# Pairwise bilinear products: where the 128 rows of a store lie in its block of the output

## The chip, the cores and the metric

The kernel runs on one core of one Trainium2 chip. Times are microseconds (us) on the device for one execution, as the median of several runs; a lower time is better.

## The reference: what is computed

`x` holds 4096 samples of 32 fields of 64 numbers, `W` is 64 x 64. Every field is multiplied by `W`, and then every pair of fields i < j gives one elementwise product, 496 pairs a sample:

```python
vid = jnp.einsum('bfd,de->bfe', x, W)
idx_i, idx_j = jnp.triu_indices(F_, k=1)
return x[:, idx_i, :] * vid[:, idx_j, :]
```

All numbers are 32-bit floats. The result has 4096 x 496 x 64 elements, 520 million bytes, against 33.6 million bytes of input.

## The kernel before, in words

**Layout.** The host gives the kernel `x` transposed: the 128 partitions are two halves of the batch times 64 numbers of a field, and a partition holds, tile by tile, 32 fields of 128 samples each. One field of one tile, 128 floats or 512 bytes in a partition, is called a unit. There are 16 tiles (`NT`), each giving 496 units of output in every partition, so 7936 units in all.

**The memory.** One buffer `mem` of 445 units a partition holds input and output. Inputs live in its low units: tiles 0 to 7 are loaded at the start, tiles 8 to 15 later as a second group (`GROUPS`, function `load`).

**The stages of a tile.** TensorE multiplies the 32 fields by a block-diagonal copy of `W` into `vid` (line 319), in two halves of 16 fields. VectorE multiplies fields of `x` with fields of `vid` (line 299), several units in one instruction, and writes the products into `mem`. The order of the pairs within a tile is by blocks (`by_block`), and the host puts them into the reference's order afterwards.

**The stores.** The 7936 units are cut into 74 slots, written out by hand in the table `SLOTS`: for each the number of units (51 to 128) and its home in `mem`. As soon as the last unit of a slot has been written, `store` (line 258) issues one DMA for it: 128 rows, one a partition, each of as many units as the slot has. The first 46 slots (`SECOND`) are issued from SP, the others from ACT; each queue takes its stores in the order of the slots. An issue waits for the semaphore `made`, which VectorE raises with each of its instructions. VectorE in turn, before it writes into units of `mem`, waits for the stores that still read them (`after`, line 201). The eight loads go through SP as well.

**The output in HBM.** It is one array of 7936 x 128 rows of one unit. Slot after slot has a block of it (`BLOCKS`), which it fills without gaps: within the block, partition p's units follow partition p - 1's. The host cuts the blocks apart and joins them again.

The function that the change touches is `store`, which hands the two sides of the DMA to `transfer` (line 194), whose line 196 issues it:

```python
rows = out[BLOCKS[slot] : BLOCKS[slot + 1], :].rearrange("(p u) c -> p u c", p=P)
transfer(rows[:, : end - begin, :], mem[:, units[0] : units[1], :], units, True, needs, act if slot >= SECOND else sp)
```

Of the kernel before, what the change touches and what calls it, by code (L numbers as in the profile page):

```python
# [10 lines left out]
P = 128  # L11

C = 128
# [27 lines left out]

SECOND = 46

PAD = 24
# [6 lines left out]
def row(n):  # L53

    return n
# [3 lines left out]
BLOCKS = [0, *accumulate(P * row(n) for n, *_ in SLOTS)]  # L59
# [112 lines left out]
def pairwise_bilinear_kernel(nc, x0, x, out):  # L172
# [8 lines left out]
    mem = ctx.enter_context(nc.sbuf_tensor([P, UNITS, C], F32))  # L181
# [8 lines left out]
    sp, act, dve = (Queue(engine, behind) for engine in (nc.sync, nc.scalar, nc.vector))  # L190
# [3 lines left out]
    def transfer(out_, in_, units, reads, needs, queue=sp):  # L194
        sem = nc.alloc_semaphore(f"moved{len(moved)}")
        queue.issue(lambda: queue.engine.dma_start(out=out_, in_=in_), needs).then_inc(sem, 16)  # L196
        queue.note(sem, 16)
        moved.append((units, reads, sem))
        return sem

    def after(units):

        needs = [(s, 16) for u, reads, s in moved if reads and overlap(u, units)]
        last = max((n for spans, n in worked if any(overlap(units, s) for s in spans)), default=0)
        return needs + [(made, last)] * (last > 0)
# [52 lines left out]
    def store(slot, last):  # L258
        nonlocal hold
        begin, end = STARTS[slot : slot + 2]  # L260
        home = SLOTS[slot][1]
        units = (home, home + end - begin)
        needs = [(made, last)]
        if hold:
            needs.append((hold[-2], 16))
            hold = []
        rows = out[BLOCKS[slot] : BLOCKS[slot + 1], :].rearrange("(p u) c -> p u c", p=P)
        transfer(rows[:, : end - begin, :], mem[:, units[0] : units[1], :], units, True, needs, act if slot >= SECOND else sp)

    for t in range(NT):
        if t in begins[1:]:
            hold = load(begins.index(t))
            for late in held:
                store(*late)
            held = []
        xs = (place_of(t, F), place_of(t, F) + F)
        blocks = list(products(by_block(), t * NP))
        for k, (at, n, nest, i, j) in enumerate(blocks):
            slot = bisect_right(STARTS, at) - 1  # L280
            begin, end = STARTS[slot], STARTS[slot + 1]
            home = SLOTS[slot][1]
            units = (home + at - begin, home + at - begin + n)
# [11 lines left out]
            needs = [(there, 2 * t + 2 - high), *after(units)]  # L295
# [9 lines left out]
            if at == end:  # L305
                late = (slot, counts[made])
                group = sum(behind <= slot for behind in STRETCHES)
                if t < begins[group]:
                    held.append(late)
                else:  # L310
                    store(*late)
# [65 lines left out]
```

How the kernel before makes its waits and increments, by code:

```python
    def issue(self, make, needs):  # L148
        needs = self.waits(needs)
        for sem, n in needs[:-1]:
            self.engine.wait_ge(sem, n)
        instruction = make()
        for sem, n in needs[-1:]:
            instruction.wait_op(sem, n, "sem-ge")
        return instruction
# [16 lines left out]
def pairwise_bilinear_kernel(nc, x0, x, out):  # L172
# [50 lines left out]
            (place + HALF, place + F + 1), False, [],  # L223
        ),
        transfer(mem[:, place : place + HALF, :], x0[:, :HALF, :], (place, place + HALF), False, []),
    ]
    work(lambda: nc.vector.memset(w2[:, :], 0.0), [], [], made)
    for half in (slice(0, D), slice(D, P)):
        work(
            lambda: nc.vector.tensor_copy(w2[half, half], mem[half, place + F, :D]),
            [(place + F, place + F + 1)], [(first[0], 16), (made, 1)], made,
        )
    nc.vector.wait_ge(made, 3).then_inc(free, 1)
    nc.vector.wait_ge(first[1], 16).then_inc(free, 1)
    owed = 0
# [67 lines left out]
            at += n  # L304
            if at == end:
                late = (slot, counts[made])
                group = sum(behind <= slot for behind in STRETCHES)
                if t < begins[group]:
                    held.append(late)
                else:
                    store(*late)
    for sem, n in sp.waits([(sem, 16) for _, _, sem in moved]):
        nc.sync.wait_ge(sem, n)
    def half(xt, lo):
        nc.tensor.wait_ge(free, 1).then_inc(free, -1)
```

## Time and profile before

| | |
|---|---|
| Median of 3 runs | 1284.6 us (1284.49 to 1284.81) |
| The profiled execution | span 1282.6 us, first to last instruction |
| VectorE busy | 1079.9 us, 273 instructions |
| TensorE busy (matmul) | 179.4 us |
| Bytes moved | 553.70 MB: 33.59 read from HBM, 520.09 written |
| Mean rate | 432 GB/s |

For the profiled execution the trace gives the span alone; the runs' median lies 2.0 us above it, which is what lies around the first and the last instruction. Read the table from the bytes: a span of 1282.6 us at 432 GB/s is all of the 553.70 MB, so data moved from the first slice to the last. VectorE is the busiest of the engines and stands still for a sixth of the span.

### The profile page before, as it was taken

To read this page: it belongs to the slowest core of one execution; us is meant where nothing else is said; L and a number is where in the kernel's file an instruction comes from. 1 tells how busy PE (TensorE), PEld (TensorE's weight loads), DVE (VectorE), ACT (ScalarE), POOL (GpSimd) and SP (SyncE) were. 2 spreads that over 40 slices of the span, in tenths; PEclk is the share of its full clock that TensorE was granted. 3 is DMA by queue.
4 is the path that set the end of the run, shared out by engine and by line. 5 is a ranking of instruction groups with operands and counts; after the bars stand their busy time and mean duration, and the time that the engine had idled before them with its cause. 6 is when DMAs were issued, how large, how long until landed. Compare 5 with 4: busy or idle time off the path is not lost. (4 is left out here: it accounts for less than half of the span.)

```text
span 1282.6 us, 1255 instructions
## 1 busy us (share of the span) xinstructions
PE 179.4 (14%) x256; PEld 70.2 (5%) x256; DVE 1079.9 (84%) x273; POOL 0.2 (0%) x4
## 2 busy tenths in 40 slices
PE   2011120301111030300020111103020020201100
PEld 1000000100000010100010000001010010100000
DVE  6589989988897989998027989989988899899980
POOL 0000000000000000000000000000000000000000
PEclk8566565756656565655565655656556575656555
DMA  9999999999999999999999999999999999999999
GB/s 404 423 435 435 438 433 433 439 435 425 435 444 429 425 437 442 428 425 446 416 426 437 426 433 436 438 434 434 439 431 442 421 437 435 427 446 429 434 425 409
DMA packets 11810, 553.70 MB, mean 432 GB/s; under 512 B 1312, under 2 KB 1312, under 8 KB 1312
## 3 DMA queue, kind: packets, MB, share of 16 engines
q1 hardware_dynamic: 7776, 340.30, 61.5%
q10 hardware_dynamic: 4032, 213.39, 38.4%
q14 instruction: 2, 0.02, 0.0%
HBM read 33.59 MB, written 520.09 MB: 432 GB/s over the span
## 5 line engine op out<-in xcount | busy, mean ns | idle before, releaser
L299 DVE TENSOR_TENSOR mem<-mem,vid 128x1024 f32<-128x1024 f32 (+11 forms) x270 | 1079.3, 4065 | 161.2 <-DMA out_dram<-mem 114.5
L319 PE MATMUL vid<-mem,w 128*128 x256 | 179.4, 866 | 1016.1 <-PEq L317 1016.1
L319 PEld LDWEIGHTS vid<-mem,w 128*128 128x128 f32 x256 | 70.2, 288 | 1124.4 <-issue 1124.4
L230 DVE COPY w<-mem 64x64 f32<-64x64 f32 x2 | 0.4, 191 | 5.1 <-DMA mem<-in_r_x_dram 5.0
L227 DVE MEMSET w<- 128x128 f32 x1 | 0.2, 165 | 0.8 <-PEq L344 0.8
L344 POOL MEMSET const-bfloat16-1.0<- 128x1 bf16 x1 | 0.1, 101 | 0.0
L344 POOL MEMSET const-uint8-127<- 128x1 uint8 x1 | 0.1, 101 | 0.0
L344 POOL MEMSET const-float32-0.0<- 128x1 f32 x1 | 0.1, 98 | 0.2 <-issue 0.2
L344 POOL MEMSET const-float32-1.0<- 128x1 f32 x1 | 0.1, 98 | 0.0
## 6 DMA issues: line engine op xcount, KB each, us to landing
out_dram<-mem ACTq DMA_DIRECT2D x9, 7680.0 KB, 23.3
out_dram<-mem SPq DMA_DIRECT2D x4, 6656.0 KB, 20.5
out_dram<-mem SPq DMA_DIRECT2D x3, 7680.0 KB, 23.1
out_dram<-mem ACTq DMA_DIRECT2D x3, 7168.0 KB, 21.5
out_dram<-mem SPq DMA_DIRECT2D x5, 4096.0 KB, 17.5
out_dram<-mem SPq DMA_DIRECT2D x3, 5632.0 KB, 18.4
out_dram<-mem SPq DMA_DIRECT2D x3, 5120.0 KB, 17.3
out_dram<-mem SPq DMA_DIRECT2D x2, 7168.0 KB, 22.6
```

The costliest lines, as they stand in the source:

```text
L227: work(lambda: nc.vector.memset(w2[:, :], 0.0), [], [], made)
L230: lambda: nc.vector.tensor_copy(w2[half, half], mem[half, place + F, :D]),
L299: lambda: nc.vector.tensor_tensor(o, left, right, ALU.mult),
L319: last = nc.tensor.matmul(vid[:, b : b + BANK, :], lhsT=w2[:, :], rhs=xt(b), start=True, stop=True)
L344: nc = _bacc.Bacc("TRN2", target_bir_lowering=False, num_devices=1, dynamic_dma_scratch_size=512)
```

## The change

The place of a row within its slot's block of the output is another. Row p is written as p = 8e + k, with e from 0 to 15 and k from 0 to 7. Before, it lay at place p of the block, that is 8e + k; now it lies at place 16k + e. The DMA's output side so has an outermost dimension of 16 (e), then one of 8 (k), then the row. The input side, 128 partitions of `mem`, is as it was. The host undoes the new order when it joins the blocks. All 74 stores are changed alike; the loads are not.

```diff
+RUN = 8
...
-        rows = out[BLOCKS[slot] : BLOCKS[slot + 1], :].rearrange("(p u) c -> p u c", p=P)
-        transfer(rows[:, : end - begin, :], mem[:, units[0] : units[1], :], units, True, needs, act if slot >= SECOND else sp)
+        rows = out[BLOCKS[slot] : BLOCKS[slot + 1], :].rearrange("(k e u) c -> e k u c", k=RUN, e=P // RUN)
+        transfer(rows, mem[:, units[0] : units[1], :], units, True, needs, act if slot >= SECOND else sp)
...
-    got = [got[a:b].reshape(P, -1, C)[:, :n] for a, b, (n, *_) in zip(BLOCKS, BLOCKS[1:], SLOTS)]
+    got = [
+        got[a:b].reshape(RUN, P // RUN, n, C).transpose(1, 0, 2, 3).reshape(P, n, C)
+        for a, b, (n, *_) in zip(BLOCKS, BLOCKS[1:], SLOTS)
+    ]
```

The program's order on SP's queue shows the forms. First the kernel before, the last two loads and the first six stores (sizes are the output side's, in elements; `in_r_x_dram` is the input):

```order
L196 DMA mem<-in_r_x_dram 128x8960
L196 DMA mem<-in_r_x_dram 128x3328
L196 DMA out_dram<-mem 128x10240
L196 DMA out_dram<-mem 128x13952
L196 DMA out_dram<-mem 128x10624
L196 DMA out_dram<-mem 128x7168
L196 DMA out_dram<-mem 128x8192
L196 DMA out_dram<-mem 128x10240
```

Then the same place in the changed kernel, where the added constant shifts the line numbers by three:

```order
L199 DMA mem<-in_r_x_dram 128x8960
L199 DMA mem<-in_r_x_dram 128x3328
L199 DMA out_dram<-mem 16x8x10240
L199 DMA out_dram<-mem 16x8x13952
L199 DMA out_dram<-mem 16x8x10624
L199 DMA out_dram<-mem 16x8x7168
L199 DMA out_dram<-mem 16x8x8192
L199 DMA out_dram<-mem 16x8x10240
```

Nothing has moved: each store is where it was, with a row as long as before, and its 128 rows are counted as 16 x 8. On ACT's queue, and on the engines, it is the same.

## Rows read from the trace of the kernel before

**Rows 1.** The page, part 1: busy us of each engine, share of the span, instructions.

```profile
span 1282.6 us, 1255 instructions
...
PE 179.4 (14%) x256; PEld 70.2 (5%) x256; DVE 1079.9 (84%) x273; POOL 0.2 (0%) x4
```

**Rows 2.** The page, part 2: DMA busy tenths and rate in 40 slices.

```profile
DMA  9999999999999999999999999999999999999999
GB/s 404 423 435 435 438 433 433 439 435 425 435 444 429 425 437 442 428 425 446 416 426 437 426 433 436 438 434 434 439 431 442 421 437 435 427 446 429 434 425 409
DMA packets 11810, 553.70 MB, mean 432 GB/s; under 512 B 1312, under 2 KB 1312, under 8 KB 1312
```

**Rows 3.** The page, part 3: DMA queues; packets, MB, share of 16 engines' span.

```profile
q1 hardware_dynamic: 7776, 340.30, 61.5%
q10 hardware_dynamic: 4032, 213.39, 38.4%
...
HBM read 33.59 MB, written 520.09 MB: 432 GB/s over the span
```

**Rows 4.** Busy time in stretches; the last two columns are DMA share and GB/s.

```profile
0.00:32.00 32.00, 8.59 (x16) 3.58 (x16) 20.28 (x9) 0.20 (x4) 0.82 0.96 404
64.00:192.00 128.00, 24.20 (x32) 9.27 (x32) 114.10 (x39) 0.00 (x0) 0.58 1.01 435
192.00:320.00 128.00, 16.87 (x24) 6.56 (x24) 119.80 (x32) 0.00 (x0) 0.58 1.01 436
320.00:448.00 128.00, 16.26 (x24) 6.39 (x24) 115.84 (x26) 0.00 (x0) 0.58 1.00 434
448.00:576.00 128.00, 23.22 (x32) 9.08 (x32) 124.14 (x25) 0.00 (x0) 0.59 1.00 434
768.00:896.00 128.00, 23.61 (x32) 9.16 (x32) 120.82 (x37) 0.00 (x0) 0.57 1.00 434
896.00:1024.00 128.00, 11.51 (x16) 4.47 (x16) 114.96 (x27) 0.00 (x0) 0.55 1.00 435
1024.00:1152.00 128.00, 22.67 (x32) 8.92 (x32) 117.51 (x31) 0.00 (x0) 0.59 1.01 435
1247.00:1283.00 36.00, 0.00 (x0) 0.00 (x0) 0.00 (x0) 0.00 (x0) 0.50 0.92 397
```

**Rows 5.** Waits of DVE, then of SP: us in total, times, longest.

```profile
DVE mem L299 <- DMA out_dram<-mem: 114.5, 35, 18.3
DVE mem L299 <- PE vid L319: 46.5, 2, 40.7
...
SPq L196 <- DVE mem L299: 695.0, 44, 48.9
SPq L151 <- DMA out_dram<-mem: 17.9, 1, 17.9
```

**Rows 6.** DMA issues: stores of the 26 slots of 128 units, median us to landing.

```profile
out_dram<-mem SPq DMA_DIRECT2D x15, 26.5
out_dram<-mem ACTq DMA_DIRECT2D x11, 25.6
```

**Rows 7.** All DMA issues of line 196: ns min/median/max of one issue; last, landing of stores.

```profile
L196 SPq DMA_DIRECT2D out_dram<-mem x46: 332/332/431, 38.5 to 773.7; - x46
L196 ACTq DMA_DIRECT2D out_dram<-mem x28: 338/338/380, 785.1 to 1247.0; - x28
L196 SPq DMA_DIRECT2D mem<-in_r_x_dram x8: 328/425/1252, 0.7 to 672.8; - x8
...
DMA to landing us min/median/max: 15.0/23.0/38.0
```

**Rows 8.** DVE at line 299, the largest shape: busy us, mean ns of one.

```profile
L299 DVE TENSOR_TENSOR mem<-mem,vid 128x16384 f32<-128x16384 f32 x5 | 86.0, 17211 | 0.0
```

## The prediction

> **What bounds the kernel now.** I read the views from the outside in: the page's engines, then the DMA slices, the queues, the stretches, the waits, and last the single DMA issues. VectorE looks busiest, 1079.9 us or 84% of the span [rows 1]. But the DMA engines stand at 9 tenths or more in every one of the 40 slices, and the rate never leaves 404 to 446 GB/s [rows 2]. The queues say it more sharply: packets of the two queues fill 61.5% and 38.4% of sixteen engines' span, 99.9% together [rows 3]. There is no idle DMA time to win. VectorE waits 114.5 us for stores, PE's product delays it for 46.5 us, and SP waits 695.0 us for VectorE to finish a slot [rows 5]; all of this lies beside transfers that go on. The bound is the time that one DMA engine (I call it a lane) needs for its rows, added up over its rows.
>
> That pace can be worked out. The second queue carries stores alone, 213.39 MB in 38.4% of 1282.6 us, which is 492.5 us: 433.3 GB/s, or 27.1 GB/s a lane [rows 3]. It hardly depends on anything. The seven stretches of 128 us give 434 to 436 GB/s with a DMA share of 1.00 to 1.01, with short slots and long ones, from SP's queue and from ACT's [rows 4]. A row of 128 units (65,536 bytes) at 27.1 GB/s takes 2.42 us.
>
> **The change, part by part.** The reshaping of the result on the host is outside the measured time. On the chip nothing is added, removed or moved: 74 stores and 8 loads are issued before [rows 7], and the order printed above keeps every one at its place and on its queue. Line and engine counts, semaphores and waits stay. Only the output side of the 74 stores changes: 128 rows become 16 x 8 rows. The loads (33.59 MB read) keep their form. An issue costs its sequencer some 0.33 us [rows 7]; even if the extra dimension doubled it, 74 x 0.33 = 24 us would lie on SP and ACT, beside the DMA, since an issue takes 23.0 us to land while the next one is already there [rows 7]. I cost that at nothing; what covers it is the rest of the store in flight, and without that cover it could cost 24 us at most.
>
> What is left is the traffic itself, and two things about it are new.
>
> First, the places. Rows 8e to 8e + 7 used to be neighbours in HBM; now the rows 8e + k of all sixteen e are. The pace in [rows 4] is the same for all slot sizes, so nothing in HBM shows as a limit now. The most that better places can give is the best stretch everywhere: 553.70 MB at 436 GB/s is 1269.9 us, 12.7 us less than the span. I take 0.
>
 No row of the trace of before shows two lanes at one port, so the price has to be bounded. From below, it is the 12.7 us gain just named. From above, every store takes twice its time. The stores are 520.09 MB [rows 3], at 433.3 GB/s 1200.3 us, so the rest of the span is 82.3 us (33.59 MB of loads at the first queue's 431.4 GB/s are 77.9 us, and gaps). Twice 1200.3 and 82.3 make 2482.9 us; the runs' median of 1284.6 us lies 2.0 us over the span, so 2484.9 us.
>
> I take a value near the upper end, because of what the evenness in [rows 2 to 4] means: the bound is a fixed pace on the way from the chip's memory to a lane, not a shared pool that averages out, and the change rearranges that very side.
>
> How near depends on how well two lanes keep step. Say that a pair shares one port for four rows, and another for the next four. If one of them leads by x rows, x of four go alone and 4 - x at half speed: 8 - x row times instead of 4. With fair sharing a lead neither grows nor shrinks. The end of the run bounds it: in the last 36 us the DMA share is 0.92 [rows 4], so lanes stand empty for 2.9 us on average, the last receipt included, or 1.2 rows of 2.42 us. So x lies between 0 and 1.2; I take a third of that, 0.4, since the receipt is part of it. The factor is 7.6 / 4 = 1.9: 1200.3 x 1.9 = 2280.6, plus 82.3, plus 2.0, is **2365 us**. With x = 1.2 the factor is 1.7, which gives 2125 us. The upper end takes the 17.9 us that SP waits at the change of the tile groups [rows 5], stores twice as slow lengthening it by as much again: 2503, rounded to 2505 us.
>
> The Trainium skill has this geometry. "DMA: Bandwidth & Descriptors", section "The descriptor swizzle", says that in a transfer of 128 partitions each engine is given two blocks of four partitions that belong to one port, with no port shared; it lists other shapes separately. "SBUF — State Buffer", section "Door 1: The DMA port swizzle", puts partitions 0 to 3 and 32 to 35 on one port, so that lanes e and e + 4 would pair, and gives 27.2 GB/s to a port; the 27.1 GB/s of a lane in [rows 3] agrees with that number, but no row shows which port it was. Its table has 64 partitions, half the ports, at 196 GB/s against 328 for all of them, for loads of 1 MiB; by that ratio of 1.67 the stores would come out at 2009 us and the whole, as an estimate, at 2093.
>
> VectorE is no second bound then: its 1079.9 us fit into 2365 us twice over. Its longest operation, 17.2 us [rows 8], delays a store only if the queue runs dry, which slower stores make rarer.
>
> **The rivals.**
> - *The lanes meet, but drift apart.* If the sharing is not fair, one lane of a pair runs ahead until it is four rows in front, and then nobody shares. For it: nothing couples the lanes but the stores' completions, and a 128-unit store takes 25.6 to 26.5 us to land where its own transfer takes 19.4 [rows 6], so a lane has some 6 to 7 us, nearly three rows, of queue to run ahead in. Against it: the same number says that there is little more, so a full four rows of lead are hard to reach. With x = 2.5 the factor is 1.375, and the time 1735 us; the case covers 1300 to 2125.
> - *No two lanes meet* (the other side: not slower). The dealing stays as it is, or a port can feed two lanes. The place is the same read side, the price 0, and it decides if a lane's 27.1 GB/s is its own limit and not that of what it reads from. For it: the queues' 99.9% cannot tell a lane's limit from a port's. Then the time is 1284.6 us, or, if neighbouring places also suit the HBM better, 1272 to 1282. The Trainium skill speaks for the latter in "DMA: Bandwidth & Descriptors", section "Latency and other measured facts": rows 512 KiB apart gave 207 GB/s a direction where a padded pitch gave 214. The trace doesn't agree that it happens here: a 128-unit slot has its rows eight apart at that distance, and the stretches that are full of such slots run as fast as the others [rows 4].
> - *Neighbouring places get in each other's way in HBM.* Sixteen lanes now write one stretch of sixteen rows. If that cost a twentieth of the stores' pace, it would be 1200.3 / 20 = 60 us, so 1345 us. Nothing in the profile speaks for it.
>
> **How the numbers follow.** Lanes meet and stay nearly in step: 0.55, with 2125 to 2505 as its own range. They meet and drift: 0.20. HBM loses: 0.05. No two meet and the time stays within 0.2% (about what a measurement of this kernel can tell from no change): 0.13. It gains: 0.07. So slower 0.80, same 0.13, faster 0.07. The forecast is the likeliest case, 2365 us. The range has to take in the first three cases to hold 8 times in 10, from 1290 to 2505 us.
>
> **What would show it.** If I am right, the DMA share stays near 1.00 in all 40 slices while the rate falls to 225 to 260 GB/s wherever stores run, and stays above 400 GB/s in the first 32 us, where loads run (404 before [rows 4]). The two queues still fill nearly the whole span. The landing of a 128-unit store goes from 26 us to over 45. VectorE's busy time stays at 1080 us and its wait for stores grows from 114.5 us to over 1000, its wait for PE all but vanishing. The forecast is wrong if packets still take 2.42 us for 65,536 bytes, that is, if the rate stays at 432 GB/s; the drift shows as a rate that climbs through the run.

## The result, and the profile after

The changed kernel takes 2159.9 us (2150.1 to 2173.6, six runs), the kernel before 1284.4 us beside it. The ratio is 1.682, with a 95% interval of 1.678 to 1.686: clearly slower, by 875.5 us.

First the page of the changed kernel: its engines, the DMA slices, the queues. They answer to [rows 1 to 3].

```profile
span 2158.7 us, 1255 instructions
...
PE 182.5 (8%) x256; PEld 71.4 (3%) x256; DVE 1082.5 (50%) x273; POOL 0.2 (0%) x4
...
DMA  9999999999999999999859998999999999999996
GB/s 372 233 290 295 251 240 262 241 237 241 251 250 250 243 250 262 273 284 295 311 165 247 276 297 216 233 242 280 245 255 247 242 258 261 231 247 250 275 282 183
...
q1 hardware_dynamic: 7776, 340.30, 57.8%
q10 hardware_dynamic: 4032, 213.39, 38.5%
```

VectorE is busy for as long as before (1082.5 us), yet the span has grown by 876.1 us. The DMA engines stand at 9 tenths nearly everywhere, as before, but what they move in a slice has fallen from 404 to 446 GB/s to 230 to 310 in most of them. So it is the packets that take longer. The stores' second queue shows it without any loads in between: 38.5% of 2158.7 us is 831.1 us for the same 213.39 MB that took 492.5 us [rows 3], a factor of 1.69.

The two queues' shares split the loss in two. Together they fill 96.3% of the span, 2078.8 us, where they filled 99.9%, 1281.3 us, before: packets are 797.5 us longer. The remaining 3.7% are 79.9 us of empty lanes, where there were 1.3. The sum, 797.5 and 78.6, is the 876.1 us.

Stretches of the changed kernel (columns as in [rows 4]; DMA share and GB/s last):

```profile
0.00:32.00 32.00, 8.64 (x16) 3.60 (x16) 20.34 (x9) 0.20 (x4) 0.82 0.96 405
60.00:90.00 30.00, 0.00 (x0) 0.00 (x0) 11.08 (x5) 0.00 (x0) 0.50 1.02 230
90.00:120.00 30.00, 6.04 (x8) 2.36 (x8) 14.61 (x4) 0.00 (x0) 0.56 0.96 243
120.00:150.00 30.00, 6.01 (x8) 2.37 (x8) 19.27 (x6) 0.00 (x0) 0.56 1.02 307
150.00:180.00 30.00, 0.00 (x0) 0.00 (x0) 22.03 (x7) 0.00 (x0) 0.50 0.92 330
180.00:210.00 30.00, 0.00 (x0) 0.00 (x0) 18.65 (x8) 0.00 (x0) 0.50 1.00 263
270.00:300.00 30.00, 0.00 (x0) 0.00 (x0) 15.81 (x6) 0.00 (x0) 0.50 0.97 235
320.00:576.00 256.00, 23.36 (x32) 9.15 (x32) 128.04 (x36) 0.00 (x0) 0.54 0.98 246
1120.00:1150.00 30.00, 0.00 (x0) 0.00 (x0) 11.18 (x5) 0.00 (x0) 0.50 0.93 206
1150.00:1180.00 30.00, 0.00 (x0) 0.00 (x0) 16.70 (x4) 0.00 (x0) 0.50 1.00 254
1180.00:1210.00 30.00, 5.11 (x8) 2.02 (x8) 20.90 (x7) 0.00 (x0) 0.61 1.01 289
1270.00:1300.00 30.00, 0.00 (x0) 0.00 (x0) 23.63 (x6) 0.00 (x0) 0.50 1.00 310
1600.00:1856.00 256.00, 19.18 (x29) 7.59 (x28) 131.28 (x36) 0.00 (x0) 0.55 0.98 250
2112.00:2158.00 46.00, 0.00 (x0) 0.00 (x0) 0.00 (x0) 0.00 (x0) 0.50 0.54 163
```

The first 32 us, full of loads, run at 405 GB/s as before (404). The stores that follow start at 230 GB/s, and the rate then climbs to 330 from the stretch at 60 us to that at 150 us. It doesn't stay there: 263 in the next stretch, 235 at 270 us. It climbs again after 1120 us, where the second group of tiles begins: 206, 254, 289, and 310 at 1270 us. In the long stretches it is near 250. At the very end the share is 0.54, so lanes finish far apart: 46 us times 0.46 is 21 us of empty lanes on average, against 2.9 before [rows 4].

The traces also keep each row's packet and each lane's landing, one by one. In the kernel before, all 1408 rows of the second queue's 128-unit stores take 2.42 to 2.46 us. In the changed kernel a quarter of them (345) still take under 2.6 us, and over half (822) take 4.4 us or more, up to 5.36: a row mostly goes at the full pace or at about half of it. The time between the first and the last of a store's sixteen landings is at most 2.0 us in all stores but one before. In the changed kernel it grows through the first eight stores, 1.1, 3.7, 6.1, 7.8, 9.7, 12.0, 13.5 and 14.9 us, then falls to 8.3; later it is up to 50. So lanes do get ahead of others, and not for good.

The waits of VectorE, and then SP's wait at the change of the tile groups, which answer to [rows 5]:

```profile
DVE mem L302 <- DMA out_dram<-mem: 933.9, 62, 45.0
DVE mem L302 <- PE vid L322: 61.1, 2, 55.2
```

```profile
SPq L154 <- DMA out_dram<-mem: 44.4, 1, 44.4
```

It waits 933.9 us for stores, where it waited 114.5: it now spends nearly as long waiting for room in the memory as working. Its two waits for PE, a short one at the start and 55.2 us at the change of the tile groups, are 61.1 us and not the 46.5 of before: at the change SP holds the loads back for 44.4 us, until the stores that still use the place have landed, where it was 17.9. (The upper end of the forecast had that wait doubled, to 36.)

And the issues of the stores, then the landing of the 26 slots of 128 units, which answer to [rows 7] and [rows 6]:

```profile
L199 SPq DMA_DIRECT2D out_dram<-mem x46: 538/538/625, 38.3 to 1276.0; - x46
L199 ACTq DMA_DIRECT2D out_dram<-mem x28: 545/546/607, 1287.4 to 2083.7; - x28
...
DMA to landing us min/median/max: 26.3/51.6/84.5
```

```profile
out_dram<-mem SPq DMA_DIRECT2D x15, 64.5
out_dram<-mem ACTq DMA_DIRECT2D x11, 55.4
```

The issue costs 0.54 us where it cost 0.33, and the landing of a 128-unit store 55 to 65 us where it took 26.

### The profile page after: what moved, and what is told of

Its sections match the earlier page's. It is cut to its first block and busy times, and to the rows that moved or that the text cites. A ratio compares the mean times of both kernels' runs of the same rounds, so it can differ in the third digit from the quotient of the medians.

```text
span 2158.7 us, 1255 instructions
## 1 busy us (share of the span) xinstructions
PE 182.5 (8%) x256; PEld 71.4 (3%) x256; DVE 1082.5 (50%) x273; POOL 0.2 (0%) x4
## 2 busy tenths in 40 slices
DMA packets 11810, 553.70 MB, mean 256 GB/s; under 512 B 1312, under 2 KB 1312, under 8 KB 1312
## 3 DMA queue, kind: packets, MB, share of 16 engines
q10 hardware_dynamic: 4032, 213.39, 38.5%
## 5 line engine op out<-in xcount | busy, mean ns | idle before, releaser
L302 DVE TENSOR_TENSOR mem<-mem,vid 128x1024 f32<-128x1024 f32 (+11 forms) x270 | 1081.9, 4068 | 995.4 <-DMA out_dram<-mem 933.9
## 6 DMA issues: line engine op xcount, KB each, us to landing
out_dram<-mem SPq DMA_DIRECT2D x4, 6656.0 KB, 35.5
```

The source lines that it names most:

```text
L302: lambda: nc.vector.tensor_tensor(o, left, right, ALU.mult),
```

## The experiments

Theory A: two lanes read through one port, because each now has eight consecutive partitions. Theory B: neighbouring places get in each other's way in HBM. The change moved two things together; the first two runs move one each.

**The dealing alone.** Rows at their old places, with gaps that keep the form of 16 x 8 rows (the gaps leave the output's content as it is; the host skips them):

```diff
-BLOCKS = [0, *accumulate(P * row(n) for n, *_ in SLOTS)]
+BLOCKS = [0, *accumulate(P * n + 16 for n, *_ in SLOTS)]
...
+        rows = out[BLOCKS[slot] : BLOCKS[slot + 1], :].rearrange("(e w) c -> e w c", e=16)
+        rows = rows[:, : 8 * (end - begin), :].rearrange("e (k u) c -> e k u c", k=8)
...
```

> The dealing of the changed kernel with the places of the kernel before: row 8e + k lies at place 8e + k again, but each group of eight rows is followed by one unit of gap, so that the output side keeps its form of 16 x 8 rows. Theory A (two lanes read through one port, since a lane has eight consecutive partitions): as slow as the change, 2100 to 2220 us. Theory B (the sixteen neighbouring places get in each other's way in HBM): the time of the kernel before, 1280 to 1300 us.

Measured: 2158.4 us, ratio 1.681 (1.676 to 1.685). Its page shows the rate and the queues:

```profile
GB/s 374 232 288 275 252 248 265 243 230 240 253 251 258 241 248 259 264 279 273 303 213 230 282 288 231 228 240 280 247 255 245 242 259 258 239 245 260 273 295 194
...
q1 hardware_dynamic: 7776, 340.30, 58.4%
q10 hardware_dynamic: 4032, 213.39, 38.4%
```

These are the changed kernel's numbers, down to the climb in the third and fourth slices. The new dealing by itself has the whole price: 2158.4 us with the old places, 2159.9 with the new.

**The places alone.** 128 rows outermost as before, each cut in eight:

```diff
+        cut = 8 if (end - begin) % 8 == 0 else 1
+        rows = out[BLOCKS[slot] : BLOCKS[slot + 1], :].rearrange("(j p u) c -> p j u c", j=cut, p=P)
...
```

> The dealing of the kernel before (128 rows outermost) with neighbouring places: a row is cut into eight pieces, and piece j of row p lies at place 128j + p, so that the lanes write one stretch at a time, about as long as in the changed kernel (slots whose units do not divide by eight stay as they were). Theory A (ports): the time of the kernel before and a few per cent for shorter descriptors, 1284 to 1330 us. Theory B (places): near the change, 1900 us or more.

Measured: 1332.8 us, ratio 1.038 (1.036 to 1.040), 2.8 us above the range given for theory A and far from B's.

**The same pieces in order** is the control that this number asked for:

```diff
-BLOCKS = [0, *accumulate(P * row(n) for n, *_ in SLOTS)]
+BLOCKS = [0, *accumulate(P * (n + (9 if n % 8 == 0 else 0)) for n, *_ in SLOTS)]
...
+        rows = out[BLOCKS[slot] : BLOCKS[slot + 1], :].rearrange("(p w) c -> p w c", p=P)
+        if cut > 1:
+            rows = rows[:, :-1, :]
+        rows = rows.rearrange("p (j u) c -> p j u c", j=cut)[:, :, : n // cut, :]
...
```

> The control for the run with the places alone: the same eight pieces a row, but at the places of the kernel before, with one unit of gap after each piece and one more after each row, so that the output side has the same form. If the 3.8% of that run are the price of the short descriptors: 1325 to 1340 us. If they are the price of neighbouring places: 1284 to 1300 us.

Measured: 1332.4 us, ratio 1.037 (1.035 to 1.039). The page's packets and queues, first with neighbouring places, then in order:

```profile
DMA packets 70946, 553.70 MB, mean 416 GB/s; under 512 B 1312, under 2 KB 1312, under 8 KB 42272
...
q1 hardware_dynamic: 43616, 340.30, 61.7%
q10 hardware_dynamic: 27328, 213.39, 38.7%
```

```profile
DMA packets 70946, 553.70 MB, mean 416 GB/s; under 512 B 1312, under 2 KB 1312, under 8 KB 42272
...
q1 hardware_dynamic: 43616, 340.30, 61.7%
q10 hardware_dynamic: 27328, 213.39, 38.7%
```

Same packets, same shares, same time to 0.4 us. So the 3.8% are the price of cutting rows, and neighbouring places cost nothing in this form. Theory B falls.

**Two halves of the partitions**, places as before and no 16 x 8 anywhere:

```diff
-        transfer(rows[:, : end - begin, :], mem[:, units[0] : units[1], :], units, True, needs, act if slot >= SECOND else sp)
+        both = [
+            (rows[part, : end - begin, :], mem[part, units[0] : units[1], :])
+            for part in (slice(0, 64), slice(64, P))
+        ]
+        transfer(both, None, units, True, needs, act if slot >= SECOND else sp)
...
```

> Places as before, but each store is two issues, partitions 0 to 63 and then 64 to 127, each with 64 rows outermost on both sides. The half issues reach half of the ports, so sixteen lanes must share them two by two, in a form without 16 x 8. Theory A (ports): slow like the change, 2050 to 2490 us. Theory B (places), and theory C (the form of 16 x 8 itself is slow to issue or to walk): 1284 to 1310 us.

Measured: 2165.3 us, ratio 1.686 (1.683 to 1.690). **The control** cuts the units in two and not the partitions:

```diff
...
+            for lo, hi in ((0, n // 2), (n // 2, n))
...
```

> The control for two issues a store: all 128 partitions in both, the first half of the units and then the second. All theories: 1284 to 1300 us, the shorter descriptors and twice the issues costing 1% at most. If it is much slower, the run with two halves says nothing on ports.

Measured: 1291.7 us, ratio 1.006 (1.004 to 1.008). Packets and queues of the two, halves of the partitions first:

```profile
DMA packets 12995, 553.72 MB, mean 255 GB/s; under 512 B 2496, under 2 KB 2496, under 8 KB 2496
...
q1 hardware_dynamic: 8512, 340.30, 57.8%
q10 hardware_dynamic: 4480, 213.39, 38.2%
```

```profile
DMA packets 22467, 553.72 MB, mean 429 GB/s; under 512 B 2496, under 2 KB 2496, under 8 KB 2496
...
q1 hardware_dynamic: 14400, 340.30, 61.6%
q10 hardware_dynamic: 8064, 213.39, 38.5%
```

The issues are as many in both. The one that reaches 64 partitions at a time is slow like the change, in a form that has nothing of it but the partitions that lanes read at one time. So it is neither the form of 16 x 8 nor its costlier issue.

**How many lanes, or where they read?** The next two runs use fewer lanes, each store waiting for the one before it:

```diff
-RUN = 8
+RUN = 64
...
-        needs = [(made, last)]
+        needs = [(made, last)] + [(sem, 16) for _, reads, sem in moved if reads][-1:]
```

> The changed kernel in step, with the output side as 2 x 64 rows (row 64e + k at place 2k + e): two lanes with 64 consecutive partitions each, which by theory A read from different halves of the ports and share none. Both theories A (ports) and D (a lane slows with the number of lanes in use, wherever they read): the lane's own pace, 27.1 GB/s: 54 GB/s in all, some 9700 us.

The other has `RUN = 32`, which makes four lanes:

> The same with 4 x 32 rows: four lanes with 32 consecutive partitions each; by theory A lanes 0 and 1 meet at every port of one half, 2 and 3 of the other, with a lead growing within a store. Theory A (ports): four lanes bring little, 27.1 GB/s times 2 to 3: 6500 to 9700 us. Without shared ports (theory D, or none): four times 27.1 GB/s, 108 GB/s, 4900 to 5000 us.

Measured: 9810.0 us with two lanes, 9170.4 with four (one run each). The rates in 40 slices, two lanes first:

```profile
GB/s 113 53 53 54 54 53 54 53 54 53 54 53 54 53 53 54 53 54 53 107 60 53 53 53 53 54 54 53 54 53 54 53 54 54 53 53 54 54 54 53
```

```profile
GB/s 122 59 61 57 56 59 58 55 57 57 59 55 58 55 57 58 55 57 56 109 69 60 57 60 56 57 57 59 57 57 56 58 58 56 57 55 57 57 56 57
```

Slices at 100 and more, and the one of 60 or 69, hold the loads. The two queues' packets fill 13.1% of sixteen engines' span (8.1 and 5.0) in the first run and 25.0% (15.0 and 10.0) in the second: two lanes of sixteen would be 12.5% and four 25.0%, so the outermost dimension does set how many lanes a store uses, and they are nearly always busy. Outside the loads two lanes move 53 to 54 GB/s, 27 each, the pace of a lane in the kernel before. Four lanes move 55 to 61 GB/s together, about 14 each. Sixteen lanes moved 433 with the old dealing, so it is not their number: a lane with partitions 0 to 31 and one with 32 to 63 share what they read through, and one with 0 to 63 beside one with 64 to 127 does not. (These two runs alone would also allow 0 to 31 to share with 96 to 127; but then the run with two halves, where all lanes read the same half, would have been fast.)

The Trainium skill says just this in "SBUF — State Buffer", section "Door 1: The DMA port swizzle": partitions p and p + 32 lie behind one port, and p + 64 behind another. The two runs agree with it; no run names the ports, nor shows which lanes pair in the changed kernel.

**Why 1.69 and not twice?** Theory A1 says that leads grow from store to store. Here every store of the changed kernel waits for the one before it (the second `needs` line above, with `RUN = 8`), so that no lead is carried on:

> The changed kernel, where each store is issued only when the store before it has landed, so that all lanes begin each store together and no lane can carry a lead over. Theory A1 (a pair shares its port, and the change is faster than twice the stores' time because leads build up from store to store): the stores come near twice their time, 1.85 to 2.0 times 1200 us, and 74 landings of 2 to 3 us each come on top: 2450 to 2700 us. Theory A2 (leads do not matter, and the sharing itself costs 1.73 times): 1.73 times 1200, 82, and the landings: 2300 to 2400 us.

And the kernel before with the same wait:

> The control: the kernel before with the same wait of each store for the one before it. Both theories: 1284 us and 74 bubbles of 2 to 4 us each, 1430 to 1600 us. The difference to the run of the change in step is what the dealing costs when no lane leads: about 1000 to 1200 us by theory A1, 870 by A2.

Measured: 2701.9 us, 1.9 above the range of theory A1, against 1393.4 us, below the 1430 given for the control. The queues, and the landing of a 128-unit store, of the change in step:

```profile
q1 hardware_dynamic: 7776, 340.30, 56.2%
q10 hardware_dynamic: 4032, 213.39, 37.3%
```

```profile
out_dram<-mem SPq DMA_DIRECT2D x15, 42.0
```

and of the kernel before in step:

```profile
q1 hardware_dynamic: 7776, 340.30, 56.9%
q10 hardware_dynamic: 4032, 213.39, 35.5%
```

```profile
out_dram<-mem SPq DMA_DIRECT2D x15, 20.7
```

The second queue's packets take 37.3% of 2701.1 us, 1007.5 us, against 35.5% of 1392.2, 494.2 us: a factor of 2.04. In the kernel before the wait leaves the packets as they were (494.2 against 492.5 us). The landing says the same, 42.0 against 20.7 us. The control's bubbles were smaller than I gave, 109 us in 74 stores or 1.5 us each, and the difference of 1308.5 us is above the 1000 to 1200 that I gave for A1 and far above the 870 of A2. It is made of 1239 us in packets (93.5% of 2701.1 against 92.4% of 1392.2) and 70 us in empty lanes. Row by row: none of the second queue's 128-unit rows is under 3.4 us now, four fifths take 4.95 us or more, and the median is 5.07. A shared row by itself takes 2.1 times its 2.42 us, and not twice.

In step, the rate doesn't climb (the stretches that showed the climb in the changed kernel):

```profile
60.00:90.00 30.00, 0.00 (x0) 0.00 (x0) 11.08 (x5) 0.00 (x0) 0.50 0.94 200
90.00:120.00 30.00, 5.59 (x8) 2.32 (x8) 14.61 (x4) 0.00 (x0) 0.52 0.91 196
120.00:150.00 30.00, 0.38 (x1) 0.00 (x0) 12.59 (x3) 0.00 (x0) 0.54 0.85 185
150.00:180.00 30.00, 5.90 (x8) 2.25 (x8) 16.12 (x6) 0.00 (x0) 0.61 0.87 188
```

**Every fourth store** waits:

```diff
+        if slot % 4 == 0:
+            needs += [(sem, 16) for _, reads, sem in moved if reads][-1:]
```

> The changed kernel where every fourth store, not every one, waits for the landing of the store before it. Theory A1 (leads that grow from store to store make the stores cheaper, so taking them away every fourth store costs): between the change and the change in step, 2250 to 2500 us. Theory A2 (leads do not matter; 18 waits cost bubbles alone): 2160 to 2200 us.

Measured: 2496.3 us, ratio 1.943 (1.939 to 1.947), at A1's upper end.

```profile
q1 hardware_dynamic: 7776, 340.30, 56.3%
q10 hardware_dynamic: 4032, 213.39, 37.6%
```

37.6% of 2494.7 us are 938.0 us for the second queue: 1.90 times 492.5. The landings of a store's lanes show why: from a store that waited to the fourth they lie some 1.2, 4.3, 7.8 and 11.9 us apart, and the next wait takes that back to 1.2. With a wait at every store they are 1.3 to 2.8 us apart throughout. So with a lead allowed over one store, four stores, or without limit, the packets' factor is 2.04, 1.90 and 1.69. What keeps the change below twice the stores' time is what these waits take away: lanes that get ahead.

**The second queue alone** has the new dealing:

```diff
...
+        if slot >= SECOND:
+            rows = rows.rearrange("(k e u) c -> e k u c", k=RUN, e=P // RUN)
+        else:
+            rows = rows.rearrange("(p u) c -> p u c", p=P)
...
```

> The change in the 28 stores of the second queue alone (213.39 of 520.09 MB); the 46 of the first as before. Theory A (ports): the price goes with the bytes dealt in the new way. The second queue's packets took 831 us in the changed kernel and 492 before, so 1284 plus 340, and up to 60 us of empty lanes: 1600 to 1700 us. The first half of the run stays at 432 GB/s.

Measured: 1645.2 us, ratio 1.281 (1.278 to 1.283).

```profile
GB/s 402 435 433 435 433 433 442 433 430 440 434 435 433 434 434 421 422 430 432 275 236 238 257 304 236 244 245 241 250 257 247 257 249 241 252 248 272 281 287 163
...
q10 hardware_dynamic: 4032, 213.39, 50.5%
```

The first half stays at the old rate and the second falls to about 250 GB/s. Its queue takes 50.5% of 1644.7 us, 830.6 us, the 831.1 of the change. The price goes with the bytes that are dealt in the new way.

## Why the prediction was right, and which term was mis-sized

- **What bounds the kernel**: right. VectorE's time stayed, and all of the loss is in packets and empty lanes.
- **Issue cost**: the extra dimension added 0.21 us an issue, 74 x 0.21 = 15 us, within the 24 us allowed and hidden, as forecast; the control with twice as many issues cost 7.6 us in all.
- **Places cost nothing**: right, for pieces of rows in the old dealing (1332.8 against 1332.4 us) and for whole rows in the new one (2159.9 against 2158.4 us).
- **Lanes meet at a port**: right, if a port is whatever two lanes read through; no run names it. The dealing alone gives 2158.4 us, and two of four lanes halve each other.
- **The factor**: here a size was off. The prediction said that "with fair sharing a lead neither grows nor shrinks", took a lead of 0.4 rows and so 1.9 times the stores' 1200.3 us. The packets are 797.5 us longer, a factor of 1.66 if all of it is the stores'. Kept in step, the pair pays 2.04, a little more than my limit of 2. But left alone it does not keep step: the landings of a store drift apart from 1.1 to 14.9 us in eight stores and the rate climbs from 230 to 330 GB/s, which is the mark that the prediction had set for the rival of lanes that drift apart. So the mis-sized term is the lead, bounded at 1.2 rows from the end of a run in which no two lanes met. By the prediction's own formula 1.66 is a mean lead of 1.3 rows, outside that bound. Its argument against drift took the queue to stay as short as before; once stores were slow it was longer, a 128-unit store landing after 55 to 65 us where in step, without a queue, it took 42.
- **Empty lanes**: missing from the sum. Lanes that lead reach the end, and the change of the tile groups, before the others: 79.9 us. The two errors partly cancel: 1200.3 x (1.9 - 1.664) = 283 us too much, 79 too little, and 2365 - 283 + 79 is 2161, against the measured 2160. That the time lies inside the forecast's own range (from 2125) is in part luck: without the empty lanes it would have been some 80 us shorter, below it.
- **What should show it**: rates of 225 to 260 GB/s in the long stretches (246 and 250 measured), loads above 400 (405), landings over 45 us (55 to 65), a DMA share near 1.00 (9 tenths in 36 of the 40 slices, less where lanes are empty) came as written. Three marks missed. The rate was to be 225 to 260 GB/s wherever stores run, and 17 of the 39 slices after the first lie outside that, from 165 to 311. VectorE's wait for stores is 934 us and not over 1000, in a run that is 205 us shorter than forecast. And its wait for PE did not vanish but grew, since at the change of the tile groups PE itself waits for loads that wait for stores.
- **The rivals**: that no two lanes meet, and that HBM loses or gains by the places, fell. Drift is real but incomplete: 2160 us lies above its 2125 and just inside the own range of the forecast, by the empty lanes. The forecast's mechanism and the drift worked together, which neither case had alone.
- **The Trainium skill's ratio** of 1.67 for 64 partitions against 128 gave an estimate of 2093 us ("SBUF — State Buffer", "Door 1: The DMA port swizzle"). In the run with two halves the second queue's packets took 1.68 times as long as before (38.2% of 2167.4 us against 492.5). The Trainium skill's number is for transfers of 1 MiB that pay their start as well (the section does not say that they are loads), and in step the factor here is 2.04, so that the two agree may well be chance.

What stays open: why one lane of a pair gets ahead, what brings the lanes together again (the rate falls from 330 to 235 GB/s by 300 us), and why a shared row takes 2.1 times its time and not twice. None was tried apart, and no trace tells which landing is which lane's.

## What to carry to other kernels

The shape that a DMA's two sides have outermost decides which partitions a lane reads, and with it which lanes meet; an edit that seems to move only addresses in HBM can take the stores from 433 to some 250 GB/s. Where queues are full and the DMA share stands at 1.00, compare the bytes that move with what one lane moves alone (27 GB/s here) before believing that the limit is the memory. Keep the 128 partitions as the outermost dimension of both sides where that can be had; if another layout of the output is wanted, cut within the row, which cost 3.7% here and not 68%.

## What the runs showed of the hardware that I had not expected

- Lanes that share what they read through drift apart when no wait holds them: 1.1 to 14.9 us between a store's landings in eight stores, 230 to 330 GB/s. A second climb, 206 to 310 GB/s, follows the change of the tile groups.
- A row moves at the full pace (2.42 us for 65,536 bytes) or, where two lanes share, at less than half of it (5.07 us in step).
- A cut row has a steady price. Pieces of an eighth raised the packets from 11,810 to 70,946, 3,696 more a lane, for 47.9 us (1332.4 against 1284.5): 13 ns each. The control with two columns, with 22,467 - 11,810 - 1,184 (the packets that signal its 74 further issues, 16 each) = 9,473 more, 592 a lane, cost 7.6 us: 13 ns again (5 to 10 us by the ratio's interval, so 8 to 17 ns).
- Waiting for each store's landing before the next is issued cost the kernel before only 109 us, 1.5 us a store.
